# A recommendation tower with gathered and one-hot tables: the same work in another order on the engines

## The reference

```python
e = stack([tbl_f[ids[:, f]] for f in range(26)], axis=1)      # 512 x 26 x 128
sd = einsum('bfd,bd->bf', e, dense)
ss = einsum('bfd,bgd->bfg', e, e)
z = concatenate([dense, sd, ss[:, iu, ju]], axis=1)           # pairs above the diagonal
h = concatenate([z, dense], axis=1)                           # 607 wide
h = maximum(h @ W_top1 + b_top1, 0)                           # 607 -> 512
h = maximum(h @ W_top2 + b_top2, 0)                           # 512 -> 256
y = h @ W_top3                                                # 256 -> 1
```

## Time and profile before

| | before |
|---|---|
| median of 3 runs | 114.46 us (114.22 to 114.61) |
| the profiled execution | 114.64 us |
| its span from first to last instruction | 112.8 us |
| TensorE busy | 104.5 us, 93% of the span |
| weight loads busy | 91.8 us, 81% |
| VectorE busy | 84.2 us, 75% |
| ScalarE busy | 67.6 us, 60% |
| GpSimd busy | 60.8 us, 54% |
| granted TensorE clock | 1.00 |

### The profile page before, as it was taken

The page is one execution under the profiler, slowest core; times in us unless marked ns, Lnnn a source line. Parts: engine busy times, 40 slices in busy tenths (PEclk is TensorE's granted clock), DMA queues, the critical chain, the costliest instruction groups (busy, mean ns, idle before and its releaser), DMA issues.

```text
span 112.8 us, 2831 instructions
## 1 busy us (share of the span) xinstructions
PE 104.5 (93%) x1095; PEld 91.8 (81%) x1095; DVE 84.2 (75%) x230; ACT 67.6 (60%) x153; POOL 60.8 (54%) x62
## 2 busy tenths in 40 slices
PE   6999999999999999499899979997999959996993
PEld 6866888888888887389799959997989949996890
DVE  4699999999999999999905891799169840885002
ACT  5545559789497387778425992768063950848120
POOL 7877777787777777776403775677257300000000
PEclk9999999999999999999999999999999999999999
DMA  2899999464999999611100122111202100000000
GB/s 72 233 269 200 242 249 265 94 210 105 325 264 328 302 259 312 155 51 47 47 9 0 47 54 71 29 47 47 52 12 58 47 6 6 0 0 0 0 6 1
DMA packets 5057, 12.75 MB, mean 113 GB/s; under 512 B 1690, under 2 KB 1818, under 8 KB 5044
## 3 DMA queue, kind: packets, MB, share of 16 engines
q1 hardware_dynamic: 3204, 8.83, 28.2%
q0 software_dynamic: 1792, 3.67, 12.3%
q10 hardware_dynamic: 48, 0.07, 0.2%
HBM read 12.56 MB, written 0.00 MB: 111 GB/s over the span
## 4 chain that ended last, share of the span: by engine, by line
PE 65%; ACT 10%; DVE 9%; DMA 7%; issue 4%; POOL 4%
PE dots L472 18%; PE dots L527 14%; PE hidden L552 12%; PE hidden L472 8%; ACT pairs L309 7%; DMA rows<-tbl,gather_idx 7%; DVE pairs L371 5%; POOL rows L269 4%; PE last_layers L451 3%; PE turned L507 2%; PE turned L552 2%; PE last_layers L576 2%; ACT h L350 2%; PE dots L445 2%; DVE onehot L378 1%
## 5 line engine op out<-in xcount | busy, mean ns | idle before, releaser
L269 POOL DMA_INDIRECT rows<-tbl,gather_idx x56 | 57.9, 1034 | 27.4 <-issue 14.8
L378 DVE TENSOR_SCALAR onehot<-ids_h 125x512 fp32r<-125x512 f16 x98 | 36.0, 426 | 0.9 <-ACT ids_h L315 0.9
L371 DVE COPY pairs<-dots 27x128 f32<-27x128 f32 (+8 forms) x88 | 23.7, 270 | 16.5 <-PE dots L527 13.8
L309 ACT COPY pairs<-dots 27x128 f32<-27x128 f32 (+8 forms) x88 | 21.0, 238 | 15.9 <-PE dots L527 13.8
L472 PE MATMUL dots<-onehot,high 125*128 125x512 f32 (+1 forms) x66 | 25.0, 399 | 0.0
L472 PE MATMUL dots<-onehot,low 125*128 125x512 f32 (+1 forms) x66 | 23.9, 381 | 0.1
L325 ACT CAST high<-table 125x1024 fp32r<-125x1024 f32 (+2 forms) x13 | 13.1, 1005 | 13.3 <-DMA table<-tbl 13.3
L527 PEld LDWEIGHTS dots<-embT 128*64 128x64 f32 x512 | 15.4, 138 | 2.8 <-issue 1.8
L527 PE MATMUL dots<-embT 128*64 128x54 f32 x512 | 15.8, 222 | 2.0 <-DVE embT L371 0.8
L386 DVE TENSOR_TENSOR low<-table,high 125x512 fp32r<-125x512 f32 (+1 forms) x24 | 16.6, 692 | 0.2 <-ACT high L325 0.2
L472 PEld LDWEIGHTS dots<-onehot,low 125*128 125x128 f32 x66 | 12.3, 188 | 2.8 <-DVE low L386 0.7
(11 more groups left out here) (55 smaller groups left out, 102.8 us busy)
## 6 DMA issues: line engine op xcount, KB each, us to landing
table<-tbl SPq DMA_DIRECT2D x10, 448.0 KB
wp<-w_pairs SPq DMA_DIRECT2D x2, 512.0 KB
rows<-tbl,gather_idx POOLq DMA_INDIRECT x56, 3.6
table<-tbl SPq DMA_DIRECT2D x1, 560.0 KB
table<-tbl SPq DMA_DIRECT2D x10, 52.0 KB
wd<-w_dense SPq DMA_DIRECT2D x1, 512.0 KB
w2s<-w SPq DMA_DIRECT2D x1, 512.0 KB
table<-tbl SPq DMA_DIRECT2D x2, 224.0 KB
```

The costliest lines, as they stand in the source:

```text
L269: pool.indirect_dma_start(out=rows[:, t % 2, n, :], out_offset=None, in_=tables[GATHERED_TABLES[n]][:, :], in_offset=bass.IndirectOffsetOn ...
L309: return nc.scalar.copy(dst, src)
L371: return nc.vector.tensor_copy(dst, src)
L378: nc.vector.tensor_scalar(onehot[i % STAGES][:, c, :], ids_h[:, i % ID_BUFFERS, :], float(c), None, ALU.is_equal).then_inc(onehot_ready, 1)
```

## The change

Only the order changes, and with it how the relu step is called. In `STEPS`: B1.2 goes behind T9 and B1.3 behind T10.0; the quarter T10.1 goes ahead of D0; B2.2 goes from ahead of D1 to behind it; L2.0, the first half of tile 2's layer 1, goes ahead of D3, with a relu of its own. Each relu is now a step of its half (`R2.0`, `R2.1`); for tiles 0 and 1 both still wait for the whole of layer 1, for tiles 2 and 3 each waits for its half. L2.1 waits for the relu of the first half, which reads the same bank. Which engine places a batch and which bank it uses stay as they are, and so does the order of the gathers.

```diff
-            T0 T1 B0.0 T2 T3 B0.1 T4 B0.2 T5 B0.3 T6 B1.0 T7 B1.1 T8 B1.2 T9 B1.3 T10.0 T11.0 B2.0
-            D0 C0.0 T10.1 T10.2 T10.3 T10.4 A10 T11.1 T11.2 T11.3 T11.4 C0.1 P0 B2.1 B2.2 A11
-            D1 C1.0 B2.3 L0.0 L0.1 R0 C1.1 P1 B3.0 M0 H0
-            D2 Y0 C2.0 V0 B3.1 L1.0 L1.1 R1 C2.1 P2 B3.2 M1 H1 B3.3
-            D3 Y1 C3.0 V1 L2.0 L2.1 R2 C3.1 P3 M2 H2
-            L3.0 Y2 V2 L3.1 R3 M3 H3 Y3 V3""".split()]
+            T0 T1 B0.0 T2 T3 B0.1 T4 B0.2 T5 B0.3 T6 B1.0 T7 B1.1 T8 T9 B1.2 T10.0 B1.3 T11.0 B2.0 T10.1
+            D0 C0.0 T10.2 T10.3 T10.4 A10 T11.1 T11.2 T11.3 T11.4 C0.1 P0 B2.1 A11
+            D1 C1.0 B2.2 B2.3 L0.0 L0.1 R0.0 R0.1 C1.1 P1 B3.0 M0 H0
+            D2 Y0 C2.0 V0 B3.1 L1.0 L1.1 R1.0 R1.1 C2.1 P2 B3.2 M1 H1 B3.3 L2.0 R2.0
+            D3 Y1 C3.0 V1 L2.1 R2.1 C3.1 P3 M2 H2
+            L3.0 R3.0 Y2 V2 L3.1 R3.1 M3 H3 Y3 V3""".split()]
...
                 elif kind == "relu1":
-                    for n in range(2):
-
-                        act.wait_ge(layer1_done, 2 * (t + 1) if t < TILES - 1 else 2 * t + 1 + n)
-                        blocks = slice(CHUNKS1 // 2 * n, CHUNKS1 // 2 * (n + 1))
-                        bank = turned if t == TILES - 1 and n == 1 else hidden[t % 2]
-                        nc.scalar.activation(h1[:, t % 2, blocks, :], bank[:, blocks, :], ACT.Relu
-                                             ).then_inc(h1_ready, 1)
+                    act.wait_ge(layer1_done, 2 * (t + 1) if t < TILES - 2 else 2 * t + 1 + i)
+                    blocks = slice(CHUNKS1 // 2 * i, CHUNKS1 // 2 * (i + 1))
+                    bank = turned if t == TILES - 1 and i == 1 else hidden[t % 2]
+                    nc.scalar.activation(h1[:, t % 2, blocks, :], bank[:, blocks, :], ACT.Relu
+                                         ).then_inc(h1_ready, 1)
...
                     if i == 0:
                         for engine in range(2):
                             pe.wait_ge(pairs_copied[engine], ALL * (t + 1))
+                    elif t == TILES - 2:
+                        pe.wait_ge(h1_ready, 2 * t + 1)
```

## The result

The changed kernel took 115.97 us in the median of its four executions (115.22, 115.78, 116.17 and one of 133.47), the kernel before 114.38. Executions like the one of 133.47, some 16 us longer, occurred with the kernel before too; the ratios leave them out, and it alone lifts this median from 115.78. The ratio is 1.0116, 95% interval [1.0059, 1.0173]: slower by 0.7 to 2.0 us. The sign was forecast, the size was not: 115.25, with a range up to 115.65.

What follows compares the result with a forecast made beforehand. VectorE was taken to bound the tables before D0 and D0 to D1, ScalarE D2 and L3.0 with VectorE close behind. Terms 0 + 0 + 0.71 + 0.07 = +0.78 us on 114.46 gave 115.25, range 114.55 to 115.65.

Steps and rivals of the forecast that it cites:

- the stall: TensorE's 1.59 us wait for a gather ahead of B1.2, before D0; its removal was forecast to gain 0.
- edit 4: L2.0 ahead of D3, relu in halves: D3 0.89 us later, L3.0 regains 0.82, net cost 0.07 us.
- Edit 1: B1.2 behind T9, B1.3 behind T10.0: the wait for the gather goes, VectorE still sets D0, gain 0.
- Edit 2: T10.1 ahead of D0: fits into TensorE's 0.5 us wait there, cost 0, at most 0.1 us.
- Edit 3: B2.2 moved behind D1: its placing on VectorE delays D2, cost 0.71 us, bounds 0.64 and 0.86.
- the stall pays: Rival: TensorE and the gather, not VectorE, set D0; removing the wait brings 1.59 us, total 113.65; chance 0.10.
- the placing is free: Rival: placing B2.2 costs VectorE nearly nothing, ScalarE sets D2; +0.51 us in all, 114.97; chance 0.08.
- edit 4 pays in full: Rival: VectorE's copies end as early as ScalarE's, L3.0 gains 1.6 us, time stays at 114.46; chance 0.06.
- The additions cost more: Rival: dearer placing, lag and products, and 0.1 us before D0; +1.25 us in all, 115.7; chance 0.06.
- three signs of being wrong: D0 starting a microsecond earlier, D2 waiting for ScalarE, or L3.0 closer to D3 than 10.8 us.

Runs made afterwards that it cites:

- e5: Kernel before with only B1.2 and B1.3 moved and T10.1 put ahead of D0, as in the change; ratio 1.0034.
- e7: The whole change, but with ScalarE instead of VectorE placing B2.2; ratio 1.0056.
- e16: The whole change run again, unaltered; ratio 1.0100 against the kernel before.
- e4: The whole change run again, unaltered; ratio 1.0099 against the kernel before.
- e6: Kernel before with only B2.2 moved behind D1; ratio 1.0084.
- e12: Kernel before with only L2.0 moved ahead of D3 with its own relu; ratio 1.0042.
- e8: e5 with the copy of the dense features moved from VectorE to ScalarE, behind its copy of T2; ratio 0.9980.
- e10: e8 with 12 products on zeros added for TensorE behind B2.1; ratio 0.9962.
- e17: The same kernel as e10, run on another chip; ratio 0.9963.
- e18: Kernel before, old order, with only the copy of the dense features moved from VectorE to ScalarE; ratio 0.9954.
- e14: The same kernel as e10, on a chip where every kernel took 131.5 us or more; no comparison.

## Why the prediction was right and where it was wrong

The mechanism was right: the stall is worth nothing, and VectorE sets D2 and L3.0. The step that failed is one term of the sum, the net cost of edit 4. It was put at 0.07 us and measured 0.32 or 0.33. The other terms missed by 0.07 us or less, in opposite directions. A second part of the miss, some 0.15 us by the ratios and more in this result's four executions, no stage of the profiles shows.

**Edit 1, gain 0: right, and shown.** Waits for VectorE's low parts took the stall's place (0.17 and 0.15 us in T11.0), D0 kept its distance to the last one-hot, and taking 0.56 us off VectorE moved D0 by 0.59. The rule of the Trainium skill that the prediction weighed (Perfetto Trace Analysis, Optimization Strategies) would have paid for the 1.59 us; here the profile after and e5 decide against it.

**Edit 2, cost 0, at most 0.1: 0.07.** D0 now stands right behind T10.1 and not behind ScalarE's copy. Transposes and quarter took 1.00 us (54.95 to 55.95) where the prediction had 0.92. The cost was given as 0 to 0.1 and entered the sum as 0.

**Edit 3, cost 0.71: measured 0.65.** The placing took 1.06 us from 74.10 and the next instruction came after 0.90, the lower of the two bounds. The overlap of 0.16 us was as forecast (0.15); the copy itself was shorter than the 1.12 us that it took at its old place. The estimate of 0.66 us for such a copy, worked out from the Trainium skill (VectorE: DVE Perf Modes, on the TRN2 errata), is too short against this row as well. e7 shows both prices that the prediction named: 0.65 with VectorE as placer, 0.44 without.

**Edit 4, net cost 0.07: measured 0.32 or 0.33.** This is the term of the sum that was mis-sized. The delay of D3 was put at 0.89 and is 1.04: from L2.0's start to D3's start 93.36 - 91.41 = 1.95 us pass, where I had taken half of the 3.57 us that 32 products need. Sixteen products span 2.02 - 0.28 = 1.74 us from first start to last, 0.116 each, and another 0.21 pass before the first dot product. The gain of L3.0 was put at 0.82 and is 0.72: VectorE's last copy ends at 104.26 and L3.0 starts at 104.40, a lag of 0.14 us, which is the lag that the prediction had read at D1; I had taken 0.06, from L3.0 behind ScalarE. So both halves missed to the dear side: the delay inside its bounds of 0.85 and 1.1 (the upper one should have been 2.05 - 0.90 = 1.15), the gain beside the 0.74 that the prediction gave for a lag of 0.14 and did not choose.

**What the sum left out.** With 1.05 instead of 0.78 the forecast would have been 115.5. The three ratios average 1.0105, or 1.2 us. The 0.15 us between are inside each interval. One more cost exists: edits 2 and 3 take work away from TensorE ahead of D1 and leave it idle for 1.90 to 2.00 us, and in e16's profiled execution the granted clock fell there and cost 1.55 us. The prediction costed that idle time at nothing and named no such rival. But the fall doesn't explain the miss. A mean granted clock of 0.985 stands beside one of the 20 executions of the whole change that took less than 130 us (result, e4, e16), and beside none of the three that make up this result. The kernel before has it in five of its 61 such executions beside the experiments. So no run shows the falls to be more frequent with the change. Of its other rivals "the stall pays" fell by e5, "the placing is free" by the 0.65 of e6, and "edit 4 pays in full" by e12. "The additions cost more", given 0.06, came nearest in value with +1.25. Of its terms the lag of 0.14 came true and the 0.1 before D0 nearly so, 16 products at 0.12 came true in part (0.13 us by its own numbers, 16 x 0.12 - 1.79, where it has 0.15), and the placing at 1.12 did not.

**The signs.** None of the three signs of being wrong appeared. D0 and D1 came at 55.95 and 66.68, outside 0.1 us of 56.33 and 67.04, and D2 at 78.94 instead of 79.3 to 79.5, mostly for the 0.45 us by which VectorE was early. D3 came 14.42 us behind D2 (14.2 to 14.3 expected) and L3.0 11.04 behind D3 (10.9 to 11.0), both outside for the term that failed.

**The range.** Its top, 115.65, lay 0.4 us above the forecast. Single executions of one kernel spread by 1 to 1.5 us here (the wait for a table load at VectorE's start took 0 to 0.88 us, the last gather up to 0.54), and a median of four carries that. With the right stages a centre of 115.5 and the same width the range would have reached 115.9, still short of the median of 115.97 and just above the 115.78 without the longest execution; how much of that is luck of four executions, the record doesn't tell.

## What to carry to other kernels

A stall of the busiest engine is worth something only if that engine is still late at the end of the stage: look at the spacing of its last instructions, and whether it is theirs or the supplier's. When a batch is moved behind a barrier, price its second half too, the copy that empties it, on the queue on which it now stands between two links of the chain; the same copy cost 0.21 us less on the engine that was waiting anyway. Splitting work across a barrier pays what the *second* engine in line allows: ScalarE was done 1.56 us earlier behind D3 (103.50 - 93.36 against 103.73 - 92.03), and L3.0 gained 0.72 of it, because VectorE was right behind.

## What the runs showed that I had not expected

- Where ScalarE and not VectorE copies the dense features, the executions with the long gather were missing. On the three chips where that was tried, 22 of 72 executions of the kernel before took 130 us or more, and none of the 42 of e8, e10, e17 and e18. In all eight profiles with a gather of 23 us it started 1.77 to 1.79 us behind the start of VectorE's copy. That the copy causes it isn't shown: the copy stands at the same place in the profiles without such a gather (0.19 or 0.20 us behind the start of another one), and e14, with the copy on ScalarE, has a gather of 20.92 us on the chip on which every kernel took 131.5 us or more. It would be worth far more than the change: some 16 us in about a third of the executions.
- The granted clock of TensorE fell from 2.4 to 1.2 GHz behind an idle time of 2.00 us in e16 (1.00, then 0.78, 0.50, 0.86 in windows of 2 us; D1 5.49 instead of 3.94 us) and behind 2.11 us in e5 (5.25 us). It stayed at 2.4 GHz behind 1.90 us in the profile after and in e4 and 1.91 us in e7 (D1 3.94 us in all three). Five executions make no rule.
- Sixteen products of 128 columns between two other groups took 1.95 us from start to the next group's start (L2.0, 91.41 to 93.36; 1.88 to 1.96 in the other profiles with L2.0 ahead of D3), thirty-two took 3.57 (71.27 to 74.84). This group, halved and put ahead of the dot products, cost more than half.
- The landing of one early table load moves the whole first half: VectorE waited for table 1's rounded part for 0 us in after and e5, 0.24 before and 0.88 in e12, and D0 came at 55.95, 55.93, 56.33 and 56.86. In e8 a wait of 0.56 took back what moving the dense copy had saved (D0 at 56.40).
